# The order of the steps of an adaLN block (selective scan and mixture of experts) and of some of its waits, on one core

## The reference

```python
h = layernorm(x) * (1 + ca) + sa
x = x + ga * attn(h)
h = layernorm(x) * (1 + cb) + sb
x = x + gb * ffn(h)

# attn: xz = rmsnorm(h) @ in_proj; xi, z = split(xz)
#       xi = silu(conv4(xi)); dt, B, C = split(xi @ x_proj); delta = softplus(dt @ dt_proj + b)
#       s[t] = s[t-1] * exp(delta * A) + delta * B * xi      (512 channels x 16 states)
#       y = sum over states of s * C, + xi * D
#       out = (y * silu(z)) @ out_proj + h
# ffn:  16 experts of width 128, the best 4 of each row weighed; a shared expert of width 256
```

## Time and profile before

| | us |
|---|---|
| median of 3 runs (lowest, highest) | 2980.88 (2977.16, 2983.09) |
| the profiled execution | 2980.19 |
| its span, first to last instruction | 2978.4 |
| busy in the span: PE, DVE, ACT, POOL | 2431.5, 2277.2, 2129.4, 2397.0 |
| mean granted TensorE clock (1 is 2.4 GHz) | 0.922 |

### The profile page before, as it was taken

The page is one execution under the profiler, slowest core; times in us unless marked ns, Lnnn a source line. Parts: engine busy times, 40 slices in busy tenths (PEclk is TensorE's granted clock), DMA queues, the critical chain, the costliest instruction groups (busy, mean ns, idle before and its releaser), DMA issues.

```text
span 2978.4 us, 52216 instructions
## 1 busy us (share of the span) xinstructions
PE 2431.5 (82%) x16084; PEld 1908.7 (64%) x16084; DVE 2277.2 (76%) x3495; ACT 2129.4 (71%) x4033; POOL 2397.0 (80%) x2382
## 2 busy tenths in 40 slices
PE   3557988888797888979888797888979788897879
PEld 1335767667576665757667575766757666676767
DVE  4777778787787878778787877878777787877753
ACT  4786877778686777868677787767868777785641
POOL 1887898889788888888888888888978878897842
PEclk7657999999899999999999899999989999998999
DMA  1775777867676785767677677776757777676841
GB/s 67 195 172 127 167 159 164 179 135 161 147 170 157 165 177 132 163 158 162 155 156 178 138 163 158 156 171 150 167 135 169 160 165 172 135 159 140 179 102 57
DMA packets 154563, 455.99 MB, mean 153 GB/s; under 512 B 22280, under 2 KB 24968, under 8 KB 154032
## 3 DMA queue, kind: packets, MB, share of 16 engines
q0 software_dynamic: 73728, 268.47, 48.2%
q1 hardware_dynamic: 80560, 184.20, 19.9%
HBM read 166.29 MB, written 17.87 MB: 62 GB/s over the span
## 4 chain that ended last, share of the span: by engine, by line
POOL 21%; issue 20%; PE 18%; DVE 15%; ACT 14%; DMA 6%; DVEq 1%; POOLq 0%; ACTq 0%; SPq 0%
POOL db_sb L669 10%; PE bank_ps L1413 8%; DVE states L1150 5%; PE moe_ps L1431 4%; POOL y_sb L681 3%; POOL act L712 3%; DMA y_sb<-c_rows 3%; DMA th_p<-x_dram 3%; ACT c_rows L886 3%; ACT da_ps L913 3%; PE rows_ps L1349 2%; DVE bank_ps L1097 2%; POOL y_sb L690 2%; DVE act L1231 2%; DVE act L1237 1%
## 5 line engine op out<-in xcount | busy, mean ns | idle before, releaser
L669 POOL TENSOR_TENSOR db_sb<-du_sb,b_sb 128x512 f32<-128x512 f32 x1024 | 1575.2, 1710 | 80.3 <-DVE states L1150 79.8
L886 ACT ACTIVATE c_rows<-rows_ps,xd_sb 128x512 f32<-128x512 f32 x1024 | 684.8, 684 | 186.4 <-PE rows_ps L1349 93.9
L1349 PE MATMUL rows_ps<-ident,states 128*128 128x128 f32 x4096 | 646.8, 291 | 177.6 <-ACT c_rows L886 104.9
L913 ACT ACTIVATE da_ps<-delta,a_sb 128x512 f32<-128x512 f32 x1024 | 704.4, 692 | 93.2 <-DVE states L1150 91.5
L712 POOL TENSOR_TENSOR act<-act,w_sb 128x256 f32<-128x256 f32 x512 | 580.8, 1185 | 224.7 <-DMA w_sb<-w_dram 119.4
L681 POOL DMA_DIRECT2D y_sb<-c_rows x512 | 608.2, 1195 | 149.9 <-DMA y_sb<-c_rows 77.1
L1431 PE MATMUL moe_ps<-eout_sb,act 128*128 128x256 f32 x2304 | 621.5, 395 | 103.8 <-POOL act L712 101.6
L1150 DVE TENSOR_TENSOR_SCAN states<-da_ps,carry,db_sb 128x512 f32<-128x512 f32 x512 | 649.3, 1276 | 54.1 <-ACT da_ps L913 52.3
L1349 PEld LDWEIGHTS rows_ps<-ident,states 128*128 128x128 f32 x4096 | 512.6, 150 | 273.8 <-DVE states L1150 123.6
L1413 PE MATMUL bank_ps<-h2T_high,ein_w_high 128*128 128x256 f16 x2304 | 643.2, 279 | 36.0 <-DVE h2T_low L1133 15.0
L1150 DVE TENSOR_TENSOR_SCAN states<-da_ps,db_sb 128x512 f32<-128x512 f32 x512 | 617.4, 1215 | 69.2 <-ACT da_ps L913 68.3
(11 more groups left out here) (169 smaller groups left out, 2633.8 us busy)
## 6 DMA issues: line engine op xcount, KB each, us to landing
y_sb<-c_rows POOLq DMA_DIRECT2D x512, 512.0 KB, 5.5
b_sb<-b_dram SPq DMA_DIRECT2D x128, 512.0 KB, 5.1
w_sb<-w_dram SPq DMA_DIRECT2D x256, 256.0 KB, 4.4
th_p<-x_dram SPq DMA_DIRECT2D x16, 512.0 KB, 8.2
r_dram<-conv SPq DMA_DIRECT2D x16, 512.0 KB, 2.8
x<-r_dram SPq DMA_DIRECT2D x16, 512.0 KB, 5.8
out_dram<-x SPq DMA_DIRECT2D x32, 256.0 KB, 2.3
mod_p<-mod_dram SPq DMA_DIRECT2D x7, 384.0 KB, 11.2
```

The lines of the kernel that those rows point to most:

```text
L669: pool.tensor_tensor(db_sb[:, n % NDB, :], du_sb[:, slots[t][0][0], b, :], b_sb[:, k % NBPAIR, s % BPAIR, :], ALU.mult).then_inc(sem["scal ...
L886: ac.activation(c_rows[:, n % NCR, j % CPAIR, :], rows_ps[j % 2][:, :], ACT.Copy, scale=xd_sb[:, slots[t][0][0], j, s:s + 1]).then_inc(sem ...
L913: ac.activation(da_ps[n % NDA][:, :], delta[:, slots[t][0][0], b, :], ACT.Exp, scale=a_sb[:, b, s:s + 1]).then_inc(sem["exp_done"], 1)
L1349: last = pe.transpose(rows_ps[j % 2][:, b * P:b * P + P], states[:, step % 2 * NB + b, j * P:j * P + P], ident[:, :])
```

## The change

Two things change. First, every constant of the planner has a new value: `LEAD_*`, `TICK`, `ROUTED`, `UNITS_END`, `SOFT`, `Z_AHEAD`, `Y_*`, `SLOT`, and all of `SHIFT`, `PLACE`, `FIRST`, `LAST` and `START`, which get more entries. Second, waits are written in another order in six operations, two are dropped where another implies them, and two are added.

```diff
-SLOT = 70.6876
-SHIFT = {"b_load": -2.314, "b_store": 0.735, "c_add": 0.79, ...
+SLOT = 70.5981
+SHIFT = {"a_made": 2.299, "b_load": -0.655, "b_store": -0.03, "c_add": 1.155, ...
...
                     def r_load(t):
+                        if nM(t) == 0:
+                            sp.wait_ge(sem["ein_low_done"], NPAIR)
...
                     def scaled(t, s, b):
+                        if n >= NDB:
+                            pool.wait_ge(sem["scan_done"], n - NDB + 1)
                         pool.wait_ge(sem[f"b_in{k % NBPAIR}"], 16 * (k // NBPAIR + 1))
...
-                        pool.wait_ge(sem["scan_done"], max(0, n - NDB + 1))
...
                     def e_weigh(t, u):
+                        pool.wait_ge(*bank_read(("expert_in", t, u)))
                         pool.wait_ge(sem[f"w_in{k % NWROWS}"], 16 * (k // NWROWS + 1))
-                        pool.wait_ge(*bank_read(("expert_in", t, u)))
...
                     def x_norm(t, half):
+                        ac.wait_ge(sem["x_rstd_done"], nP(t) + 1)
                         ac.wait_ge(*bank_room(key))
-                        ac.wait_ge(sem["x_rstd_done"], nP(t) + 1)
...
                     def z_tanh(t, j):
+                        if nM(t) == 0:
+                            ac.wait_ge(sem["ein_low_done"], NPAIR)
...
                     def tap(t, b, k):
-                        v.wait_ge(sem["halo_set"], n + 1)
-                        v.wait_ge(sem["xi_centered"], n + 1)
-                        v.wait_ge(sem["tapped"], (CONV - 1) * n + k)
+                        if k:
+                            v.wait_ge(sem["tapped"], (CONV - 1) * n + k)
+                        else:
+                            v.wait_ge(sem["xi_centered"], n + 1)
+                            v.wait_ge(sem["halo_set"], n + 1)
...
                     def dt_low(t):
-                        v.wait_ge(sem["dt_high_done"], 2 * nP(t) + 1)
+                        v.wait_ge(sem["dt_high_done"], 2 * nP(t) + 2)
...
                     def dtp(t, b):
+                        pe.wait_ge(*bank_read(("xd", t)))
                         pe.wait_ge(sem["dt_high_done"], 2 * nP(t) + 2)
-                        pe.wait_ge(*bank_read(("xd", t)))
...
                     def rows(t, s, j):
-                        pe.wait_ge(sem["scan_done"], (step + 1) * NB)
-
                         before = (step, j - 2) if j >= 2 else (step - 1, j + 2)
+                        if j == 0:
+                            pe.wait_ge(sem["scan_done"], (step + 1) * NB)
                         if before[0] >= 0:
                             pe.wait_ge(*c_scales(*before))
+                        if j > 0:
+                            pe.wait_ge(sem["scan_done"], (step + 1) * NB)
```

More of the change, by code:

```diff
@@ L137, in mix_steps @@
     return out
[L140 to L143, removed]
-SLOT = 70.6876
[L145 to L154, removed]
-         "x_load": -2.297, "x_norm": 0.671, "x_rstd": -0.656, "x_scale": 0.42, "x_stat": 0.151, "xd": 0.045, "xd_evac": 0.152,
-         "xd_t": 0.072, "xd_t_evac": 0.855, "xi": 0.112, "xi_center": 0.256, "xi_copy": 0.112, "y_evac": 0.386, "y_gate": -0.101,
-         "y_t": 0.622, "z": -0.763, "z_gate": -0.93, "z_tanh": -0.773}
@@ L160 @@
-PLACE = {"b_load_0": 0.173, "b_load_3": -0.295, "b_load_4": 0.013, "b_load_7": 1.807, "c_scale_2": 0.046, "carry_0": -0.001,
[52 rows of a table removed]
-FIRST = {"b_store": 0.125, "dt_bias": 0.034, "dt_high": -0.092, "dtp": 0.026, "ein_low": -4.541, "h_rms": 0.889, "h_scale": 0.293,
-         "hn_high": -0.177, "hn_low": -1.03, "in_low": -1.842, "r_add": -0.475, "soft_ln": -0.603, "tap": 0.219, "u_tanh": 1.112,
-         "x_load": 0.132, "x_rstd": 5.921, "x_scale": -0.544, "xi": 2.127, "xi_copy": 0.024}
-LAST = {"e_mul": -0.008, "e_weigh": -0.199, "expert_in": -0.512, "expert_out": -0.749, "h2_high": 0.25, "h2_low": 0.658, "h2_t": 0.387,
-        "op_gate": -0.447, "out_add": 0.012, "r_load": -3.075, "w_load": 0.015, "w_store": -2.166, "w_t": -0.691, "x1_norm": -0.005,
-        "x1_rstd": -1.397, "x1_stat": 0.167, "y_evac": 0.514, "z": -0.362}
@@ new lines @@
+FIRST = {"b_store": -1.691, "delta": -7.942, "dt_bias": -5.55, "dt_high": 0.322, "dt_low": 0.284, "dtp": -0.316, "du": 15.142,
+         "ein_high": 2.29, "ein_load": 1.427, "ein_low": -2.424, "h_rms": -7.043, "h_scale": -2.667, "h_square": 0.779, "hn_high": -2.392,
+         "hn_low": -2.331, "hn_t": -1.045, "in_high": 9.103, "in_low": -7.464, "r_add": -2.869, "r_gate": -3.859, "r_store": 9.187,
+         "skip": 0.46, "skip_evac": 7.151, "skip_t": 2.867, "soft_exp": 3.454, "soft_ln": 1.178, "tap": 0.991, "u": 2.33, "u_tanh": 0.596,
+         "x_load": -1.459, "x_norm": 0.639, "x_rstd": -0.049, "x_scale": 0.35, "x_shift": 0.09, "x_stat": 2.908, "xd": -5.521,
+         "xd_evac": -1.259, "xd_t": 0.226, "xd_t_evac": -0.902, "xi": -4.74, "xi_center": 1.94, "xi_copy": -0.671}
@@ new lines @@
+LAST = {"e_act": -0.086, "e_mul": 0.001, "e_tanh": 0.024, "e_weigh": 5.36, "expert_in": 0.948, "expert_out": 1.413, "h2_high": 1.147,
+        "h2_low": -2.551, "h2_scale": -1.666, "h2_t": -3.41, "logit": 1.396, "logit_exp": 0.191, "op": -0.871, "op_gate": 0.209,
+        "out_add": 1.16, "out_gate": 0.978, "out_store": -0.147, "r_load": 1.398, "router": 0.022, "w_evac": -1.369, "w_load": 2.655,
+        "w_store": 2.436, "w_t": 0.633, "x1": 0.207, "x1_norm": -3.031, "x1_rstd": -2.619, "x1_stat": 0.228, "y_evac": 0.006,
+        "y_gate": -0.421, "y_t": -0.772, "z": -3.279, "z_gate": -0.688, "z_tanh": -0.619}
```

29 lines of the change are left out of this document (27 added, 2 removed), and 122 rows, old and new, of the table PLACE.

## The result

The kernel after takes 2879.9 us (median of 4 runs, 2877.2 to 2881.3) beside 2981.9 for the kernel before on the same chip (2977.2 to 2983.1): ratio 0.966, with an interval of 0.964 to 0.968, or 102 us less. The forecast was 2946 us, with a range down to 2895. The direction was right, the size was not: the gain lies 15 us outside the range.

What follows compares the result with a forecast made beforehand. With four engines nearly equally busy, the wait that ends last was taken as the bound. Slot terms 0.6 x (21 + 30) = 31 us, plus 1 and 2.5, made 34.5 off 2980.2: 2946 us, range 2895 to 2992.

Steps and rivals of the forecast that it cites:

- The reading of the bound: Middle slots: four engines similarly busy, POOL idle 26.5 of 175.8 us; the wait ending last decides, not one engine's work.
- x_load ahead of w_load_15: Slot end, SP's list: input load issued 6 us earlier, saving 1.6 us in each of 13 slot ends, 21 us.
- The first scans and z: Slot start on DVE: scans ahead of z_gate_2 and z_gate_3 fill idle time, 2.0 us in 15 slots, 30 us.
- The slower rival: Slot start: z_gate_0 ahead of x_scale_0 waits for its z_tanh, delaying it 2.1 us a slot; 3009 us, chance 0.20.
- Does that reach the end of the slot?: Factor 0.6 for how much of the slot-end and first-scan savings passes through to the slot's end, giving 31 us.
- c_add one scaled earlier, carries later, the other moves: Mid-slot reorderings on POOL and SP should rarely block and SP's three reordered DMAs meet no waiting reader; 0 us.
- w_evac earlier: On ACT: weights stored earlier, but e_weigh_2's wait for DVE's e_mul_2 hides it; 0, at most part of 4.43 us.
- The wait on the instruction itself: Reordered waits: 0.07 us saved for each wait moved onto the instruction that ends last; 1 us in all.
- Slot 0: First slot: earlier h_scale and earlier xi_copy in the convolution, less dt_low's cost; 2.5 us, bounds 0 and 5.
- The middle of the slot gains too: Rival: half of POOL's 10.0 us a slot waiting for w_sb and e_mul goes, 45 us more; 2901 us, chance 0.17.

Runs made afterwards that it cites:

- e2: As e1, with only x_load moved ahead of w_load_15 at the thirteen slot ends; ratio to the kernel before 0.9961, 15 us less than e1.
- e1: Kernel before's places on every engine, with the changed kernel's waits; ratio to the kernel before 1.0013.
- e11: e3 plus all engines' new places from scan 13 of a slot to scan 1 of the next; ratio to the kernel before 0.9883.
- e3: As e1, with the new places in SP's list alone; ratio to the kernel before 0.9839, 52 us less than e1.
- e15: The whole change with the slot's start (z, z_tanh, z_gate, x_norm, x_scale, x_shift, first four scans, exps, scaleds) as before; ratio to the kernel before 0.9638.
- e6: As e1, with only w_load_9 ahead of out_store_0 and w_load_10 ahead of b_load_7; ratio to the kernel before 0.9896, 35 us less than e1.
- e7: The whole change except SP's list, which is that of before; ratio to the kernel before 0.9824, 49 us more than after.
- e16: The whole change with w_load_9 behind out_store_0 and w_load_10 behind b_load_7 again; ratio to the kernel before 0.9816, 46 us more than after.
- e5: As e1, with only w_load_2 and w_load_3 ahead of b_load_4, w_load_5 and b_store ahead of b_load_5; ratio to the kernel before 0.9969.
- e10: e3 plus all engines' new places before scan 7 of each slot; ratio to the kernel before 0.9736.
- e13: e3 plus e_weigh_2 and e_weigh_3 at their new places on POOL; ratio to the kernel before 0.9826.
- e14: The whole change with e_weigh_2 and e_weigh_3 at their places of before; ratio to the kernel before 0.9643.
- e8: All new places, with the six operations' waits in their old order; ratio to the kernel before 0.9665.
- e9: e3 plus all engines' new places from scan 7 of a slot to its end; ratio to the kernel before 0.9842.
- e17: e10 with POOL's list of before; ratio to the kernel before 0.9957, 35 us slower than e3.
- e18: e3 plus the new places from scan 3 to scan 7 of each slot; ratio to the kernel before 0.9832.
- e4: As e1, with the new places in POOL's list alone; ratio to the kernel before 1.0506, 147 us slower than e1.

## Why the prediction was wrong, step by step

**The reading of the bound** held. POOL's idle time was what could be won, and it fell by what the slot did. DVE's, ACT's and POOL's busy times hardly moved, PE's fell by 3.0 us a slot.

***x_load ahead of w_load_15*** was right in size. The forecast was 1.6 us in each of 13 slot ends times 0.6, 12 us; e2 measured 15 (11 to 20), and its slot is 1.7 us shorter, of which 1.0 lies in the slot end. SP, POOL and DVE in order of time, kernel after, at the end of slot 8:

```profile
1401.00 1.21 SPq L571 DMA_DIRECT2D b_sb<-b_dram  x1
1402.30 0.42 SPq L594 DMA_DIRECT2D th_p<-x_dram  x1
1406.56 0.32 SPq L587 DMA_DIRECT2D w_sb<-w_dram  x1
```

```profile
1412.19 0.90 POOL L713 DMA_DIRECT2D y_sb<-c_rows  x1 [2.88 <-DMA y_sb<-c_rows]
1412.80 1.74 POOL L744 TENSOR_TENSOR act<-act,w_sb 128x256 f32<-128x256 f32 x2
1417.06 0.89 POOL L713 DMA_DIRECT2D y_sb<-c_rows  x1 [2.52 <-DMA y_sb<-c_rows]
1417.67 1.04 POOL L744 TENSOR_TENSOR act<-act,w_sb 128x256 f32<-128x256 f32 x1
```

```profile
1410.67 1.28 DVE L1186 TENSOR_TENSOR_SCAN states<-da_ps,carry,db_sb 128x512 f32<-128x512 f32 x1
1411.86 0.40 DVE L1102 BATCH_NORM_STATS2 bn<-th_p 128x6 f32<-128x256 f32 x1
...
1422.55 0.69 DVE L1199 SCALAR_TENSOR_TENSOR zg<-zg,bank_ps 128x512 f32<-128x512 f32 x1 [1.20 <-ACT zg L960]
...
1430.92 0.69 DVE L1199 SCALAR_TENSOR_TENSOR zg<-zg,bank_ps 128x512 f32<-128x512 f32 x1 [1.51 <-ACT zg L960]
```

`x_load` is 1.3 us behind `b_load_0` and 4.3 ahead of `w_load_15`, `x_stat` starts as the scan ends, and the waits before `e_weigh_35` and `x_rstd` are gone. The 4.77 us before `c_add_14_1` are now 2.88 and 2.52 us before two `c_add`s. The step said "the 4.77 mostly stays", and it does: as means, the waits before `c_add_14_0` and `c_add_14_1` together are 4.5 us in e1 and 4.3 in e2. In the kernel after they are 5.7, while the 0.9 us before `e_weigh_34` are gone. Why the slot end keeps its length all the same is the 1.0 us by which the engines' new places lengthen it (e11 against e3); these waits do not add up to it, and what does stays open.

***The first scans and z*** failed: forecast were 30 us times 0.6, and e15, which takes the new order back, loses nothing. The gaps before the `z_gate`s were real; in the new order DVE idles 1.20 and 1.51 us before the first and the third. The scans won a place and no time. In the chain that ended last of the kernel after, from 1400 to 1430 us, stand only POOL's operations, the issues between them and the DMAs of its `c_add`s, and no `z_gate`. The slower rival, `z_gate_0` ahead of `x_scale_0`, has its 1.20 us, and in the whole change no cost of it could be told either.

***Does that reach the end of the slot?*** One factor stood for two stretches and for waits of different kinds. The runs show no such factor: it is about 1 for `e_weigh_22` and not to be told from 0 for `e_weigh_2` and for the `z_gate`s.

***c_add one scaled earlier, carries later, the other moves*** is the step that failed most. It named three DMAs of SP (`r_store`, `b_store`, `b_load_4`) that "meet no reader that waits". It left out `w_load_9` and `w_load_10`, which pass `out_store_0` and `b_load_7`, though their reader's 66.2 us stood in the earlier trace rows. By e3, e6, e7 and e16 SP's list is worth some 50 us and this pass 35 to 46 of them; it was costed at 0. `w_load_2` and `w_load_3`, which pass `b_load_4` in e5's piece, had a reader that waits too; that piece measured 13 us. Of what the other engines' lists give beside SP's new one, 53 us, e10 measured 31 in the first half; that was in no term either, and which steps carry it stays open.

***w_evac earlier*** was costed at 0 because "`e_weigh_2` then waits for DVE's `e_mul_2`", by the 4.43 us that the earlier trace rows put down to DVE. The trace before says otherwise once DVE and SP are read beside it:

```profile
1517.54 0.42 DVE L1237 TENSOR_TENSOR act<-act,bank_ps 128x256 f32<-128x256 f32 x1
```

```profile
1514.61 0.33 SPq L547 DMA_DIRECT2D w_dram<-wT  x1
1518.43 0.81 SPq L557 DMA_DIRECT2D w_sb<-w_dram  x2
```

`e_mul_2` ended at 1517.96, 3.7 us before `e_weigh_2` began at 1521.64; what landed last was `w_load_0`, issued at 1518.43 and landed at 1521.58. As means over slots 4 to 14, in us from the slot's start:

```
              w_evac ends  w_load_0 issued  e_mul_2 ends  e_weigh_2 starts
before            44.2          46.8            48.1           50.7
e13               44.5          47.5            48.4           52.1
e10               42.0          43.6            50.2           50.4
after             42.8          44.4            51.0           51.2
```

So with `w_evac` ahead of `exp_4_0` on ACT the weights do come earlier, and then `e_mul_2`, moved back, sets the step. The cover named for the 0 was not the cover. Whether `w_evac` alone gains was not tried; e13 and e14 warn that this wait's going by itself is worth nothing.

***The wait on the instruction itself*** was forecast at 1 us gained; e1 and e8 show none, and their intervals are wider than that.

***Slot 0*** was forecast to end 2 to 3 us earlier. The first `du` begins at 69.50 instead of 73.84:

```profile
69.50 4.96 POOL L688 TENSOR_TENSOR du_sb<-delta,u_sb 128x512 f32<-128x512 f32 x4 [41.39 <-DVE delta L1160]
```

That is 4.3 us, but executions differ: in the 13 profiles with slot 0's old order on all engines (before, e1 to e3, e5, e6, e9 to e13, e17, e18) it begins between 71.7 and 74.0 us, at 72.9 as a mean, and in the five with the new order (after, e7, e8, e14, e16) between 69.5 and 70.2, at 69.9. So the order is worth 3.0 us, as forecast. The terms were sized otherwise, though. From the first `xi_center` to the fourth it takes 14.8 us before, 13.7 in e1 and 11.1 after, where 3 us less were forecast; `h_scale` begins 2.4 us earlier, but the first `xi_center` only 0.2. And the two `in_low`s cost less and not more: the first took 2.11 us beside another POOL instruction, the second 1.27, 3.4 together against 4.7 before.

**The rivals.** "The middle of the slot gains too" had the right place and its mark came true, but it took half of the waits times 0.6 on top of a slot end of which 18 us never came. The whole account of POOL's waits in the middle slots, in us a slot: 6.4 less for `w_sb` and `e_mul` (10.0 to 3.6), 1.6 less before `du` for `delta`, 0.4 less for `c_scale`s, 2.1 more for scans (48.8 / 10.6 = 4.6 to 74.0 / 11.0 = 6.7) and 1.2 more for the `c_add`s' landings. That leaves 5.1 of the 6.2 by which its idle time fell. The range ended at 2895 because the rival counted only half of the 10.0 us, times 0.6. Its error was to bound waits by a share instead of asking of each which list sets it and whether the change moves that list.

## What to carry to other kernels

An in-order queue that issues DMAs for several readers is a list like an engine's. For each reader's wait on a landing, find when the DMA was issued and what stood ahead of it in the queue, and then look through the diff for that pair; here it was one DMA held back 13.6 us by a store and another load that it did not need, at 2 to 3 us in each slot. A removed wait is worth its length only if what the engine meets next is ready: `e_weigh_22` gave all of its 2.3 us and `e_weigh_2` none of its 3.9 that could be told, and only a run with that one move told them apart. A stretch that keeps its length can hide a gain and a loss: only the runs with one of the two showed them. Last, where the change moves both ends of a pair (`c_add` and `c_scale`, `e_weigh` and `e_mul`), a list moved alone measures the broken pair: 147 us lost in e4.
